# Identity products placed in TensorE's queue during the first attention and its routing (57 of 512 columns)

## The reference

```python
Sim = (enc @ w1)[:, :, None] + (dec @ w2)[:, None, :] + einsum('bid,bjd->bij', enc * w3, dec) + b_sim[0]
A = softmax(Sim, axis=2)
hq_hat = einsum('bij,bjd->bid', A, dec)
Batt = softmax(max(Sim, axis=2), axis=1)
hc_hat = einsum('bi,bid->bd', Batt, enc)[:, None, :]        # broadcast over i
x = x + concat([enc, hq_hat, enc * hq_hat, enc * hc_hat], -1) @ W_qv + b_qv
...
top_vals, top_idx = top_k(layernorm(x) @ Wg + bg, 2)        # two experts of eight for each token
x = x + sum over the two experts of softmax(top_vals) * ((h * silu(g)) @ W2 + b2)
```

## Time and profile before

| | |
|---|---|
| runs | 1209.14, 1210.71, 1213.11 us; median 1210.71 |
| the profiled execution's own time | 1212.98 us |
| its span in the trace | 1211.2 us |
| mean granted TensorE clock | 0.898 of full |
| busy: PE, PEld, DVE, ACT, POOL | 84%, 66%, 60%, 53%, 47% of the span |
| share of the chain that ended last: PE, DVE, POOL, DMA, ACT | 59%, 16%, 7%, 5%, 5% |

### The profile page before, as it was taken

The page is one execution under the profiler, slowest core; times in us unless marked ns, Lnnn a source line. Parts: engine busy times, 40 slices in busy tenths (PEclk is TensorE's granted clock), DMA queues, the critical chain, the costliest instruction groups (busy, mean ns, idle before and its releaser), DMA issues.

```text
span 1211.2 us, 21764 instructions
## 1 busy us (share of the span) xinstructions
PE 1021.6 (84%) x6596; PEld 797.6 (66%) x6596; DVE 729.0 (60%) x2451; ACT 641.7 (53%) x2115; POOL 573.6 (47%) x923
## 2 busy tenths in 40 slices
PE   3894899857899988968999997697599999976993
PEld 3884788744555577855777765686467777655993
DVE  5458244477777684267676777622876766754443
ACT  2215223245878843428887875233487888831231
POOL 5112566534000024458555666657475555664452
PEclk9865899977999987989999999688799999975997
DMA  2002356676920014120000000274300000013666
GB/s 64 13 18 87 117 169 197 207 167 163 406 93 2 27 49 119 63 69 19 1 19 2 19 1 25 65 210 144 87 19 1 2 1 1 2 40 115 196 204 192
DMA packets 116003, 102.83 MB, mean 85 GB/s; under 512 B 18027, under 2 KB 97571, under 8 KB 115888
## 3 DMA queue, kind: packets, MB, share of 16 engines
q1 hardware_dynamic: 104992, 82.45, 23.0%
q0 software_dynamic: 8448, 17.20, 4.4%
q10 hardware_dynamic: 2448, 1.80, 0.6%
HBM read 65.04 MB, written 36.36 MB: 84 GB/s over the span
## 4 chain that ended last, share of the span: by engine, by line
PE 59%; DVE 16%; POOL 7%; issue 6%; DMA 5%; ACT 5%; SPq 1%; DVEq 0%; POOLq 0%; ACTq 0%
PE ps L2872 5%; PE ps L2690 4%; PE ps L2886 4%; PE ps L2692 4%; PE ps L2770 4%; PE ps L2691 4%; PE ps L2783 3%; PE ps L3060 3%; PE ps L2900 2%; PE ps L3398 2%; PE ps L3411 2%; DMA xr<-xr_d,src_i 2%; PE ps L3402 2%; POOL xq_d L883 2%; PE ps L3216 2%
## 5 line engine op out<-in xcount | busy, mean ns | idle before, releaser
L1278 ACT ACTIVATE ex<-ps,nmx 128x154 f32<-128x154 f32 x512 | 194.4, 392 | 69.8 <-DVE nmx L2199 68.2
L1065 POOL TENSOR_TENSOR pp<-ex,rc 128x256 f32<-128x256 f32 x256 | 157.6, 616 | 145.7 <-DVE rc L2204 144.9
L2199 DVE TENSOR_REDUCE nmx<-ps 128x2 f32<-128x308 f32 x256 | 119.6, 470 | 61.5 <-PE ps L2692 60.9
L2872 PEld LDWEIGHTS ps<-ident,pp 128*128 128x128 f32 x640 | 74.0, 142 | 57.5 <-POOL pp L1066 50.2
L902 POOL DMA_INDIRECT yq_d<-yq,ids_q x78 | 74.7, 957 | 74.5 <-DVE yq L1961 55.2
L2690 PE MATMUL ps<-kp,q_s 128*128 128x308 f32 x256 | 96.5, 377 | 15.3 <-ACT ex L1278 8.2
L1278 ACT ACTIVATION_READ_ACCUMULATOR ex<-ps,nmx 128x1 f32 x512 | 105.0, 205 | 0.0
L2872 PE MATMUL ps<-ident,pp 128*128 128x128 f32 x640 | 100.6, 281 | 4.8 <-POOL pp L1066 4.7
L1402 ACT ACTIVATE pe<-ps,nmx 128x154 f32<-128x154 f32 x256 | 84.6, 396 | 27.7 <-DVE nmx L2080 26.8
L872 POOL TENSOR_TENSOR ln_r<-ln_v,mhalf 128x4 f32<-128x4 f32 x32 | 34.7, 1083 | 99.3 <-DVE ln_v L1696 81.3
L2531 DVE SCALAR_TENSOR_TENSOR h_r<-ps,bias_r,g_r 128x256 f32<-128x256 f32 (+1 forms) x92 | 34.6, 437 | 75.0 <-ACT g_r L1560 63.5
(11 more groups left out here) (446 smaller groups left out, 2784.2 us busy)
## 6 DMA issues: line engine op xcount, KB each, us to landing
w_r<-in_L_ffn_W SPq DMA_DIRECT2D x69, 256.0 KB, 3.5
xq_d<-blankq SPq DMA_DIRECT2D x4, 4160.0 KB, 23.1
w_q<-in_L_ffn_W SPq DMA_DIRECT2D x46, 256.0 KB
w_q<-in_L_ffn_w SPq DMA_DIRECT2D x46, 128.0 KB
xq<-xq_d SPq DMA_DIRECT2D x22, 130.0 KB, 2.9
w_s<-in_L_ffn_W SPq DMA_DIRECT2D x8, 256.0 KB
w_e<-in_L_ffn_W SPq DMA_DIRECT2D x8, 256.0 KB, 4.8
acc<-yq_d SPq DMA_DIRECT2D x8, 256.0 KB, 4.4
```

The source lines that it names most:

```text
L1065: pool.tensor_tensor(pp[st % 2][:, m % 4, 2 * j:2 * j + 2, :], w[:, :, 0:P], r.broadcast_to([P, 2, P]), ALU.mult)
L1278: ins = act.activation(ex[:, tt % NEX, j, :], ps[:, tt % 3, j * SK:(j + 1) * SK], ACT.Exp, bias=nmx8[:, tt % 8, j:j + 1], accum_out=sm8[:, ...
L2199: dve.tensor_reduce(nmx8[:, tt % 8, :], ps[:, tt % 3, 0:2 * SK].rearrange("p (h s) -> p h s", h=2), AX.X, ALU.max, negate=True).then_inc(n ...
L2872: last = pe.transpose(ps[:, bank, k * P:(k + 1) * P], pp[st % 2][:, k, c, :], ident[:, :])
```

## The change

A new helper `idle_products(bank, count)` issues `count` products of the bfloat16 identity with itself, repeated four times along the columns, so each is a 128x128 weight load and a product of 512 columns, and fills one PSUM bank. No semaphore is waited for and none is raised. There are nine calls, all in the list that orders `sorted_runs`: 4, 5, 2 and 3 products into bank 7 before the first `features_out` writes it, and 5, 2, 12, 8 and 16 into bank 0 after ACT has copied the last turned tokens out of it and before the next step writes it. That is 57 products of 512 columns. Nothing else is added, removed or moved, and no other engine's program changes.

```diff
--- before.py
+++ after.py
@@ -2664,6 +2664,11 @@
                 for b in range(B):
                     xT_of(s, b)
 
+            def idle_products(bank, count):
+
+                for _ in range(count):
+                    mm(ps[:, bank, :].rearrange("p (a c) -> p a c", a=4), ident_bf[:, :], ident_bf[:, :].rearrange("p (a c) -> p a c", a=1).broadcast_to([P, 4, P]), start=True, stop=True)
+
             def tail_sum(l, b, *ready):
 
                 wait(pe, *held_by(l, ("f", b)))
@@ -3431,14 +3436,18 @@
                 xT_of(0, 1)
                 similarities(0)
                 xT_of(0, 2)
+                idle_products(7, 4)
                 maxima_row(0)
                 xT_of(0, 3)
+                idle_products(7, 5)
                 maximum_out(0)
                 turn_weights(0, 0)
+                idle_products(7, 2)
                 attended(0, 0)
                 batch_sums(0)
                 similarities(1)
                 turn_weights(0, 1)
+                idle_products(7, 3)
                 maxima_row(1)
                 attended(0, 1)
                 maximum_out(1)
@@ -3460,6 +3469,7 @@
                 batch_sums(2)
                 attended(2, 0)
                 attended(2, 1)
+                idle_products(0, 5)
                 maxima_row(3)
                 xT_of(1, 1)
                 maximum_out(3)
@@ -3467,6 +3477,7 @@
                 turn_weights(3, 0)
                 features_out(2)
                 choices(1)
+                idle_products(0, 2)
                 batch_sums(3)
                 turn_weights(3, 1)
                 attended(3, 0)
@@ -3475,13 +3486,16 @@
                 features_out(3)
                 xT_of(1, 2)
                 choices(2)
+                idle_products(0, 12)
                 rank(2)
                 xT_of(1, 3)
                 choices(3)
+                idle_products(0, 8)
                 count()
                 rank(3)
                 biases()
                 lists()
+                idle_products(0, 16)
                 columns(0)
                 columns(1)
                 hidden_run(0)
```

## The result

| | before | with the change |
|---|---|---|
| median of 5 runs, us | 1212.02 (1209.14 to 1213.11) | 1204.66 (1203.06 to 1206.45) |
| ratio, 95% interval | | 0.9933 (0.9913 to 0.9953) |
| span of the profiled execution, us | 1211.2 | 1202.4 |
| mean granted clock | 0.898 | 0.912 |

The change makes the kernel some 8 us faster, 0.7%. The page of the changed kernel, as the earlier trace rows: its span, TensorE's row, and the clock in 40 slices of 30 us.

A forecast was written before the change was run, and what follows sets the result against it. TensorE was taken as busiest, its granted clock at half in several stretches. Terms -4.4 - 4.7 + 1.3 + 0.3 - 1.5 = -9.0 us gave 1204.0 or 1201.7; forecast 1202.5 us, range 1196.5 to 1209.

The forecast's parts named there:

- Step 1: 28.0 to 38.0 us, through `similarities(1)`: fillers in three waits hold the clock, -4.4 us.
- Step 2: 65.4 to 75.6 us: five products fill the wait of 1.52; if the clock holds, -4.7 us.
- the third rival: The win is taken back: falls have another cause or come elsewhere, as after 49 us; 1209, chance 0.12.
- the second rival: Second listed: everything held, -14.5 us, chance 0.12; the sense fits the first listed: second stretch not held, about 1207, 0.24.
- Step 3: 79.0 to 89.2 us: clock lost again ahead of `features_out(3)`, 0; 2.6 us more if it holds.
- Step 4: 92.6 to 120 us: eight products at half clock delay `count`, +1.3 us; twelve partly at half clock delay `rank(2)`, +0.3.
- Step 5: 119.6 to 130.8 us: sixteen products hide in the wait and raise the clock for the first expert products, -1.5 us.
- The rival by the Trainium skill: Only the two long waits matter, since shorter ones before 90 us keep the clock; some -1.5 us, part of 0.12.

The follow-up runs named there:

- the first fourteen: The change with only its first four groups (4, 5, 2, 3 products) kept and the last five removed; ratio 0.9976 to the kernel before.
- the 57 others: The change plus 20 products in three new places (6, 6, 8), less its groups of eight and twelve; ratio 0.9920 to the kernel before.
- insurance: The change plus 20 products in three new places, less its group of eight, with five more around the narrow products; ratio 0.9928 to the kernel before.
- the kernel before, again: The kernel before, unchanged, traced a second time on the chip of the first experiments; 1252.0 us there, the traced run 1260.38 us.
- 57 narrow products: The change with all 57 products in place but 8 columns wide instead of 512; ratio 1.0007 to the kernel before.
- the last group alone: The change with all groups removed except the sixteen products ahead of the first expert run; ratio 0.9967 to the kernel before.

## Why the prediction was right, and where it was off

The forecast was 1202.5 us, -9.0 on the profiled execution; measured were 1204.66 and a ratio that is worth 8.1 us. The same point of the program, the end of F, stands at 130.61 us in the trace before and at 122.40 in the changed one, -8.2: A to F save 8.6, and the changed kernel's first turning of tokens started 0.4 later (17.27 for 16.88 us).

- **Price of one product**: 0.25 and 0.50 us taken, 0.22 and 0.43 measured. The Trainium skill's 215.7 and 426.7 ns ("TensorE: Matmul & The Clock Gate", section "Wait — 56ns, not 53.3ns?") were nearer than my scaling by columns; the trace agrees with them.
- **Step 1, -4.4**: measured -4.37 (A, 21.40 to 17.03). A is 17.03 to 17.05 in every kernel that had the first four groups at full width and size, and 20.26 to 21.65 in the five traces in which they did not hold the clock or were not there. That the fillers bridge the two waits, and that what is behind comes earlier with `similarities(1)`, is shown by the first fourteen alone: the clock stays up until 48.0 us and `features_out(2)` starts 3.5 us earlier.
- **Step 2, -4.7**: this is the term that was mis-sized. B gave -2.6 (44.94 to 42.31), or -2.0 to -2.1 against the second trace of the kernel before. The step had it that the clock holds from there on if five products fill the wait of 1.52. It does not hold by them: in one trace it fell at 49.2, behind the wait of 1.58 that no filler fills (the place that the third rival named), and at 59.4 behind logits and averages of one to eight columns with TensorE busy for 6.80 of 6.80 us; in the other at 63.9, behind narrow products and two waits of 0.45 and 0.34 us. The size was about right for a clock that holds: with the 57 others B is 40.59, -4.35, and with insurance 40.98. So the outcome lay between the forecast and the second rival, and the fall at 49.2 was a piece of the third.
- **Step 3, 0**: the first trace shows -1.3, but the kernel before, again, and the one with 57 narrow products have C at 5.76 too. What changed is where in `features_out(3)` the clock came back. The mechanism was right: it was lost at 76.5, just ahead of `features_out(3)` at 76.60, and six products behind `rank(1)` gave 1.6 us.
- **Step 4, +1.3 and +0.3**: right in sign, and too dear. The eight ran at half clock and overran, as said, but `count` came only 0.44 and 0.57 us later behind `choices(3)`: they cost 3.4 us and not 4.0, and `count` behind them ran at full clock. For the twelve +0.3 was taken and 0 is what taking them out shows.
- **Step 5, -1.5**: -0.5 in F in the first trace, where the clock fell again at 120.9, -1.3 to -1.7 in the second and with the last group alone; and 0.2 to 0.5 in E.

So -4.4, -2.6, -1.3, +0.8, -0.5, -0.5 make -8.6 in the first trace (unrounded) where -9.0 was forecast. That they come so near is partly luck: step 2 gave 2.1 less than forecast, and that is nearly made up by the 1.3 of step 3, which is not the change's, and by step 4, which cost 0.8 less. The mechanisms of steps 1, 3 and 5 stand; in step 2 the clock did not hold as long as was put, and in step 4 the price was too high.

Behind 124.3 us nothing was expected to change. The traces end 8.8 us apart, but in between the distance of the same DVE instruction goes from 4.8 to 9.6 us, with other falls of the clock at other points. That the end agrees with the forecast in these two traces is luck too; that the kernel is faster rests on the ratios of many runs.

The rival by the Trainium skill ("TensorE: Matmul & The Clock Gate", section "Why this matters for your kernels") is refuted: waits of at most 1.6 us, filled or not, decided between 24 and 34 us whether the clock stayed up, in every trace. (The prediction's "any before 90 us" holds from 17 us on; TensorE's waits of 9.36 and 3.74 us lie before that.)

## What to carry to other kernels

Where a chain of short dependent steps keeps TensorE waiting for a microsecond at a time, work without use in exactly those waits can be worth much (here 8 of 113 us), if the steps behind are TensorE's own; price it as free up to the wait's end and at its full time beyond, and fill nearly the whole wait: doubled groups gave most of the gain back, and products of half the width lost the clock at 32 us. Read the wait at the clock that the filler will have there: fillers at half clock need twice the room, and one that runs cold ahead of a step on the chain costs. Look too at stretches that count as busy with narrow products, for the clock was lost there with no wait at all, and take two traces before crediting a saving to an edit.

## What the runs showed of the hardware that was not expected

- The clock's records begin only some 22 to 25 us into the span. Before that the page shows 1.00 while products run at the slow pace (first row).
- The points at which the clock changes move against the program from one execution to the next: it fell at 49.2, 59.4 and 76.5 us in one trace of the changed kernel, at 63.9 and 77.6 in another. With such moves stretch C differs by 1.2 us between the two traces of the kernel before, and stretch F by 0.7 between those of the change.
- The kernel before takes 1212 us in the first comparison, 1213 on one chip, 1252 to 1254 on another and 1263 on a third. A to F are nearly the same in both traces of it (113.73 and 112.81), so the difference lies behind them: 1080.6 us from the end of F in the one, 1128.5 in the other. Its cause is open.
